# A four-block fp32 chain on one Trainium2 core: the last recurrence over tiles 0 to 7, and slots from a scan

## The chip, the cores and the metric

The kernel runs on one core of one Trainium2 chip. The metric is the device time of one execution in microseconds, from the first to the last instruction with what lies around them; lower is better. It was timed in three executions, and profiled in one more.

## The reference

2048 tokens (4 batches of 512) with 512 features pass four blocks, each added to its input with a gate: an expert MLP chosen by token id, a Hadamard-rotated MLP of width 2048, a decaying recurrence over time, and a routed MLP. The change touches the last two:

```python
# block 3, per batch and feature, over time: k = layernorm(x), v = ctx
no = max(o, u + k); A = exp(o - no); E = exp(u + k - no)
y = (A * p + E * v) / (A * q + E)
# then p, q, o are carried on with decay w
x = x + tanh(g_xattn[1]) * y
# block 4, on xf = layernorm(x)
scores = softmax(xf @ gate_w)
sel = top_k(scores + expert_bias, 2)               # two of 8 experts
order = argsort(sel.reshape(-1), stable=True)      # rows sorted by expert
routed_in = xf[order // 2] * scores_of_sel[order]
h = silu(ragged_dot(routed_in, w1)) * ragged_dot(routed_in, w3)
out = silu(xf @ sw1) * (xf @ sw3) @ sw2            # shared expert
out[order // 2] += ragged_dot(h, w2)
```

## The kernel before

The order of every engine's work is written out by hand; semaphores join the engines. Each engine runs its own queue strictly in order, so an instruction that waits holds all behind it. Tokens lie in 16 tiles of 128. Products are made from a high and a low fp32r part of both factors, three groups of matmuls each.

**The last recurrence and the shared expert share one stage**, the loop `for t in range(TT)` on every engine. A tile t passes: `d_x_shared` (TensorE transposes tile t+1 into bank 0, ScalarE copies the high part dxh and normalizes a later tile into xsd, VectorE subtracts for dxl), `d_up` (24 matmuls, L1332, into banks 2 and 3; it waits for the gate product dmid of tile t-1), the gate (ScalarE's `dsg`, L970, then VectorE's `dmid`, L1731), `d_mid` (transposes of dmid, with dhh on ScalarE and dhl on VectorE) and `d_down` (12 matmuls, L1367), two tiles behind.

Between them lie the four units (128 features each) of the last batch's recurrence, numbers 12 to 15. The table at L39, `KEY_T, VALUE_T, BACK_T`, says in which tile each passes its steps:

- KEY: TensorE transposes the normalized rows xnc (`c_keys`, L1203), VectorE's `front` runs a scan (L1621) and a difference (L1624) into cd, ScalarE's `spread` splits cd in two (L864, L865), GpSimd's `limit` makes a third part (L669).
- VALUE: TensorE transposes values (`c_values`), ScalarE's `exps` makes three exponentials (L882 to L884, with a table load before them, and another before the next dsg), VectorE's `sums` makes five instructions (L1633 to L1639), GpSimd adds (L673), VectorE's `invert` takes a reciprocal (L1643), and GpSimd's last product (L677) gives the unit's output. In GpSimd's queue unit n's L673 and L677 (`finish`) stand before `limit(n + 1)`. ScalarE's `c_norm` makes xnc of the next unit, four instructions at L874, in the same tile.
- BACK: TensorE transposes the output into bank 5 (`c_back`, L1215), and VectorE's `add_out` adds it to the residual (L1649).

On VectorE a tile's order is: `d_x`, `sums`, `d_mul` (dmid), `front`, `add_out`, `d_hid`, `invert`.

Tiles 8 to 15 take their router logits from plain fp32 products (`d_router`, L1344) into columns of bank 5: tiles 8 to 11 at the end of t = 4 to 7, and tiles 12 to 15, whose rows the recurrence ends, in t = LATE = 9. In a tile of BACK_T the router product first waits until `add_out` has read bank 5:

```python
                if HELD - 4 <= t < HELD:
                    if t in BACK_T:
                        pe.wait_ge(s_co, NU - DC + BACK_T.index(t) + 1)
                    d_router(t + 4)
```

**From router to slots.** In tile LATE + 1 VectorE makes softmax and top two (`scores`, `choice`), ending in mask1 (L1768). In tile LATE + 2 TensorE counts, for every token and expert, the tokens ahead of it in 18 matmuls with a triangle and ones (L1384 to L1388), and `places` on VectorE (L1776 to L1797) makes of it each row's slot in the sorted buffer; its last instruction frees the routed part. VectorE's `rows` then makes 32 scaled row tiles (L1615; 4 in tile LATE + 2, then 4 and 3 in each tile), and GpSimd stores each with one indirect DMA (L739). SyncE waits for all 32 and then loads the first routed tile; TensorE waits for it before its last shared `d_down`. Behind the 32 stores GpSimd's queue has the weights of the second expert, and on from there each expert's weights (L593 loads, L600 splits), paced by TensorE's tiles. The routed part has 39 tiles, and the program ends with the gathers of both results.

## Time and profile before

| | |
|---|---|
| three runs | 1429.71, 1430.18, 1434.71 us; median 1430.18 |
| the profiled execution | 1426.54 us, span 1424.9 us, mean granted TensorE clock 0.964 |
| TensorE matmul | 1278.3 us busy, 90% |
| VectorE | 640.9 us, 45% |
| ScalarE | 447.2 us, 31% |
| GpSimd | 384.5 us, 27% |
| chain that ended last | TensorE 61%, issue 14%, GpSimd 10%, DMA 10%, VectorE 3% |

Busy time is each engine's own and overlaps with the others'. The profiled execution ran 3.6 us faster than the median of the timed ones; times read from the trace belong to the former. In the timeline each line gives the start, the time until the end of the group, the engine, the line of the kernel, the operation with its tiles, and in brackets how long the engine had been idle before and what released it. The stage described above runs from about 821 to 995 us, the routed part from 1009 to about 1384 us.

### The profile page before, as it was taken

To read this page: it belongs to the slowest core of one execution; us is meant where nothing else is said; L and a number is where in the kernel's file an instruction comes from. 1 tells how busy PE (TensorE), PEld (TensorE's weight loads), DVE (VectorE), ACT (ScalarE), POOL (GpSimd) and SP (SyncE) were. 2 spreads that over 40 slices of the span, in tenths; PEclk is the share of its full clock that TensorE was granted. 3 is DMA by queue.
4 is the path that set the end of the run, shared out by engine and by line. 5 is a ranking of instruction groups with operands and counts; after the bars stand their busy time and mean duration, and the time that the engine had idled before them with its cause. 6 is when DMAs were issued, how large, how long until landed. Compare 5 with 4: busy or idle time off the path is not lost.

```text
span 1424.9 us, 18510 instructions
## 1 busy us (share of the span) xinstructions
PE 1278.3 (90%) x6269; PEld 1078.1 (76%) x6270; DVE 640.9 (45%) x1066; ACT 447.2 (31%) x755; POOL 384.5 (27%) x314
## 2 busy tenths in 40 slices
PE   3489989999999999999999979999699999998670
PEld 3378877888888888888888868887588888886660
DVE  5423336554436755665465466665132222223116
ACT  1223334333325432543244347542122222222110
POOL 2400011100002311231234142337555220035454
PEclk9999999999999999999999989999799999999795
DMA  8632246564557875794865231235787562257747
GB/s 278 215 101 76 88 137 235 214 227 171 204 192 272 292 281 202 268 338 183 276 265 218 84 85 45 74 116 219 219 229 213 148 192 77 74 158 214 184 136 254
DMA packets 103941, 265.60 MB, mean 186 GB/s; under 512 B 11004, under 2 KB 44872, under 8 KB 91592
## 3 DMA queue, kind: packets, MB, share of 16 engines
q1 hardware_dynamic: 69480, 165.13, 32.6%
q0 software_dynamic: 33968, 99.40, 22.9%
q8 instruction: 37, 0.61, 0.2%
q10 hardware_dynamic: 432, 0.26, 0.1%
q14 instruction: 24, 0.20, 0.0%
HBM read 182.97 MB, written 81.79 MB: 186 GB/s over the span
## 4 chain that ended last, share of the span: by engine, by line
PE 61%; issue 14%; POOL 10%; DMA 10%; DVE 3%; ACT 1%; SPq 1%; POOLq 0%; DVEq 0%; ACTq 0%
PE bank L1166 25%; PE bank L1194 12%; POOL W L600 6%; PE bank L1332 5%; DMA W<-in_L_ffn_w 5%; PE bank L1101 4%; PE bank L1082 4%; PE bank L1121 2%; PE bank L1367 2%; DMA xs_sorted<-xn,slot 1%; POOL fin_low L761 1%; PE bank L1138 1%; POOL xs_sorted L739 1%; DMA fin_high<-y_all,slr 1%; PE bank L1133 1%
## 5 line engine op out<-in xcount | busy, mean ns | idle before, releaser
L1166 PE MATMUL bank<-xTh,G 128*128 128x512 f32 x1024 | 278.5, 397 | 1.8 <-DVE xTl L1577 1.8
L1166 PEld LDWEIGHTS bank<-xTh,G 128*128 128x128 f32 x1024 | 188.8, 188 | 42.6 <-issue 3.4
L1332 PE MATMUL bank<-W,dxh 128*128 (+2 forms) x880 | 203.2, 374 | 0.0
L1332 PEld LDWEIGHTS bank<-W,dxh 128*128 128x128 f32 x880 | 170.2, 193 | 15.7
L1194 PE MATMUL bank<-DN,bhh 128*128 128x512 f32 x512 | 158.2, 390 | 0.0
L1332 PE MATMUL bank<-W,dxl 128*128 (+2 forms) x440 | 116.1, 387 | 29.5 <-POOL W L600 16.6
L1166 PE MATMUL bank<-xTl,G 128*128 128x512 f32 x512 | 137.5, 390 | 0.0
L600 POOL TENSOR_TENSOR W<-wst,W 128x1792 fp32r<-128x1792 f32 (+1 forms) x24 | 101.6, 4233 | 90.5 <-DMA W<-in_L_ffn_w 89.1
L1731 DVE TENSOR_TENSOR dmid<-bank,dsg 128x448 f32<-128x448 f32 x55 | 34.3, 623 | 197.9 <-ACT dsg L970 197.8
L1599 DVE SCALAR_TENSOR_TENSOR bs<-bank,tab,bs 128x512 f32<-128x512 f32 x64 | 47.5, 743 | 161.1 <-PE bank L1166 161.1
L1367 PE MATMUL bank<-W,dhh 112*128 (+1 forms) x440 | 112.6, 398 | 0.0
L1194 PEld LDWEIGHTS bank<-DN,bhh 128*128 128x128 f32 x512 | 96.2, 188 | 21.5 <-issue 1.7
L1166 PEld LDWEIGHTS bank<-xTl,G 128*128 128x128 f32 x512 | 96.1, 188 | 20.9
L1332 PEld LDWEIGHTS bank<-W,dxl 128*128 128x128 f32 x440 | 81.8, 196 | 37.8 <-issue 30.5
L970 ACT ACTIVATE dsg<-bank 128x448 f32<-128x448 f32 x55 | 30.0, 545 | 241.4 <-PE bank L1332 241.4
L1194 PE MATMUL bank<-DN,bhl 128*128 128x512 f32 x256 | 103.7, 405 | 0.0
L1367 PEld LDWEIGHTS bank<-W,dhh 112*128 112x128 f32 x440 | 83.8, 190 | 20.1
L858 ACT ACTIVATE bhh<-bs 128x512 fp32r<-128x512 f32 x64 | 40.3, 630 | 185.3 <-DVE bs L1599 185.3
L1723 DVE TENSOR_TENSOR dxl<-bank,dxh 128x512 fp32r<-128x512 f32 x55 | 37.9, 688 | 113.1 <-ACT dxh L952 113.0
L852 ACT ACTIVATE bs<-bank,tab 128x512 f32<-128x512 f32 x64 | 44.1, 689 | 136.5 <-PE bank L1166 136.5
L529 POOL TENSOR_TENSOR rstd<-vare,cst 128x4 f32<-128x4 f32 x16 | 17.3, 1081 | 230.3 <-DVE vare L1498 230.2
L980 ACT ACTIVATE dys<-bank 128x512 f32<-128x512 f32 x55 | 32.9, 598 | 114.5 <-PE bank L1367 114.5
(229 smaller groups left out, 1960.0 us busy)
## 6 DMA issues: line engine op xcount, KB each, us to landing
G<-gate_up_split SPq DMA_DIRECT2D x48, 1024.0 KB, 7.0
DN<-down_split SPq DMA_DIRECT2D x24, 1024.0 KB, 4.9
wst<-in_L_ffn_w POOLq DMA_DIRECT2D x24, 896.0 KB, 5.6
W<-in_L_ffn_w POOLq DMA_DIRECT2D x24, 896.0 KB, 7.6
gate_up_split<-G SPq DMA_DIRECT2D x16, 1024.0 KB, 7.4
y_all<-dys SPq DMA_DIRECT2D x55, 256.0 KB, 2.0
xs_sorted<-zero POOLq DMA_DIRECT2D x3, 3328.0 KB, 20.9
xsd<-xs_sorted SPq DMA_DIRECT2D x39, 256.0 KB, 3.4
```

What stands on the lines that cost most here:

```text
L600: pool.tensor_tensor(w_place(Wl, slot, p, width), w_rows(p, width), f32(w_place(Wh, slot, p, width)), ALU.subtract)\
L852: act.activation(bs[g % 2][:, :], bank[0][:, :], ACT.Silu, scale=tab[:, T_WGT + g % NK:T_WGT + g % NK + 1]).then_inc(s_bs, 1)
L858: act.activation(bhh[g % 2][:, :], bs[g % 2][:, :], ACT.Copy).then_inc(s_bhh, 1)
L1082: mm = pe.matmul(bank[2 + par][:, :], a[par][:, k, :], w[:, bass.ds(ex[par] * DC + k, 1), :], start=(n == 0), stop=(n == 3 * DC - 1))
L1101: mm = pe.matmul(bank[4 + par][:, :], a[par][:, k, :], w[:, bass.ds(ey * DC + k, 1), :], start=(n == 0), stop=(n == 3 * DC - 1))
L1166: mm = pe.matmul(bank[m][:, :], G[:, c % 2, f, h, m, i, :], a[b % 2][:, i, :], start=(n == 0), stop=(n == 3 * DC - 1))
L1194: mm = pe.matmul(bank[2 + i][:, :], a[g % 2][:, i * P:(i + 1) * P], DN[:, c % 2, f, h, :], start=(k == 0 and n == 0), stop=(k == NK - 1 an ...
L1332: mm = pe.matmul(bank[o][:, 0:width], a[par][:, k, :], w[:, bass.ds(slot, 1), at + k * step:at + k * step + width].rearrange("p a n -> p ( ...
L1367: mm = pe.matmul(bank[4][:, :], a[par][:, k, :], w[0:HP, bass.ds(slot, 1), W_2 + k * D:W_2 + (k + 1) * D].rearrange("p a n -> p (a n)"), s ...
L1599: dve.scalar_tensor_tensor(out=bs[g % 2][:, :], in0=bank[1][:, :], scalar=tab[:, T_WUP + g % NK:T_WUP + g % NK + 1], in1=bs[g % 2][:, :], ...
L1723: dve.tensor_tensor(dxl[t % 2][:, :, :].rearrange("p k n -> p (k n)"), bank[0][:, :], f32(dxh[t % 2][:, :, :]).rearrange("p k n -> p (k n) ...
L1731: dve.tensor_tensor(dmid[t % 2][:, :], bank[3][:, 0:HID], dsg[:, :], ALU.mult).then_inc(s_dmid, 1)
```

## The change

Five edits go together.

1. The recurrence's tables: unit 14 has its keys in tile 3, not 4, and unit 15 in tile 5, not 6; the last output comes back in tile 7 instead of 8.
2. LATE is 8 instead of 9: router tiles 12 to 15, scores, mask, slots and rows all come one tile sooner. `xn_next` keeps ScalarE's normalizing of later tiles in step, and `rows` stops at 32.
3. ScalarE makes xnc of the next unit in the tile of KEY, behind `spread`, not in the tile of VALUE.
4. On VectorE `d_mul` stands ahead of `sums`.
5. mask1 lies expert by expert. A scan with resets counts a token column's hits up to each tile, a subtraction gives those before it, and TensorE needs three matmuls instead of 18.

```diff
--- before.py
+++ after.py
@@ -36,7 +36,7 @@
 LOWEST = -1.0e38
-KEY_T, VALUE_T, BACK_T = (0, 2, 4, 6), (1, 3, 5, 7), (2, 4, 6, 8)
+KEY_T, VALUE_T, BACK_T = (0, 2, 3, 5), (1, 3, 4, 6), (2, 4, 5, 7)
@@ -44,7 +44,7 @@
 HELD = 8
-LATE = 9
+LATE = 8
 NT1 = 2 * TT + E1 - 1
@@ -53,7 +53,7 @@
     ("up", 5), ("router", 8), ("up", 6), ("router", 9), ("up", 7), ("router", 10), ("up", 8), ("router", 11),
-    ("up", 9), ("up", 10), ("router", 12), ("router", 13), ("router", 14), ("router", 15)] + [("up", t) for t in range(11, TT)]
+    ("up", 9), ("router", 12), ("router", 13), ("router", 14), ("router", 15)] + [("up", t) for t in range(10, TT)]
 NTURN = len(TURNS)
@@ -187,9 +187,9 @@
         dmid, dhh, dhl, dys = (dmid0, dmid1), (dhh0, dhh1), (dhl0, dhl1), (dys0, dys1)
-        wst1, wst2, row, sel1, mask1, base1, nt1, tend1, tst1, tex1, tex1_i, tend1_i, slf, slw, slr, rsc = run(
-            WKV, ("wst1", [P, 2048]), ("wst2", [P, 2048]), ("row", [P, 4, D]), ("sel1", [P, TT, E1]), ("mask1", [P, TT + 1, E1]),
-            ("base1", [P, TT + 1, E1]), ("nt1", [P, E1]), ("tend1", [P, E1]), ("tst1", [P, E1]), ("tex1", [P, 48]),
+        wst1, wst2, row, sel1, reset, mask1, upto1, base1, nt1, tend1, tst1, tex1, tex1_i, tend1_i, slf, slw, slr, rsc = run(
+            WKV, ("wst1", [P, 2048]), ("wst2", [P, 2048]), ("row", [P, 4, D]), ("sel1", [P, TT, E1]), ("reset", [P, E1, TT]), ("mask1", [P, E1, TT]), ("upto1", [P, E1, TT]),
+            ("base1", [P, E1 * TT + E1]), ("nt1", [P, E1]), ("tend1", [P, E1]), ("tst1", [P, E1]), ("tex1", [P, 48]),
             ("tex1_i", [P, 48], I32), ("tend1_i", [P, E1], I32), ("slf", [P, 2, TT]), ("slw", [P, 2, TT], I32),
@@ -951,18 +951,22 @@
+            def xn_next(q):
+                if q + 2 < NTURN and TURNS[q + 2] != ("router", HELD + 4):
+                    xn(q + 2)
             def d_x_shared(t):
...
                 d_x(q, t % 2, t - 1)
-                if q + 2 < NTURN and t != LATE:
-                    xn(q + 2)
+                xn_next(q)
...
                 act.activation(dxr[t % 2][:, :, :].rearrange("p k n -> p (k n)"), bank[0][:, :], ACT.Copy).then_inc(s_dxr, 1)
-                xn(q + 2)
+                xn_next(q)
@@ -995,6 +999,8 @@
                     spread(NU - DC + KEY_T.index(t))
+                if t in KEY_T[:-1]:
+                    c_norm(NU - DC + KEY_T.index(t) + 1)
                 if t == LATE:
@@ -1005,8 +1011,6 @@
                     d_x_router(HELD + 7)
-                if t in VALUE_T[:-1]:
-                    c_norm(NU - DC + VALUE_T.index(t) + 1)
                 if t >= 2:
@@ -1379,14 +1383,13 @@
                 if t == LATE + 2:
                     pe.wait_ge(s_mask1, 1)
-                    w = (TT + 1) * E1
-                    pe.matmul(bank[5][:, 0:w], tri, mask1[:, :, :].rearrange("p i e -> p (i e)"), start=True, stop=False)
-                    for j in range(TT):
-                        pe.matmul(bank[5][:, (j + 1) * E1:w].rearrange("p (i e) -> p i e", e=E1), ones,
-                                  mask1[:, j:j + 1, :].broadcast_to([P, TT - j, E1]), start=False, stop=False, skip_group_check=True)
-                    pe.matmul(bank[5][:, 0:w].rearrange("p (i e) -> p i e", e=E1), ones,
-                              mask1[:, TT:TT + 1, :].broadcast_to([P, TT + 1, E1]), start=False, stop=True).then_inc(s_rank1, 1)
+                    w = E1 * TT
+                    pe.matmul(bank[5][:, 0:w], tri, mask1[:, :, :].rearrange("p e i -> p (e i)"), start=True, stop=False)
+                    pe.wait_ge(s_mask1, 2)
+                    pe.matmul(bank[5][:, 0:w], ones, pb[:, :, :].rearrange("p i e -> p (i e)"), start=False, stop=True)
+                    pe.matmul(bank[5][:, w:w + E1], ones, upto1[:, :, TT - 1], start=True, stop=True).then_inc(s_rank1, 1)
                 if t == 0:
@@ -1741,7 +1744,8 @@
                 dve.tensor_copy(lg[:, HELD + 4:TT, :].rearrange("p i e -> p (i e)"), bank[5][:, 4 * E1:(TT - HELD) * E1]).then_inc(s_lr, 1)
-                dve.memset(mask1[:, :, :], 0.0)
+                chain(dve.memset(reset[:, :, :], 1.0))
+                chain(dve.memset(reset[:, :, 0:1], 0.0))
                 dve.wait_ge(s_lr, 5)
@@ -1765,7 +1769,14 @@
                 chain(last)
-                dve.tensor_tensor(mask1[:, 0:TT, :], sel[0][:, :, :], sel[1][:, :, :], ALU.add).then_inc(s_mask1, 1)
+                dve.tensor_tensor(mask1[:, :, :].rearrange("p e i -> p i e"), sel[0][:, :, :], sel[1][:, :, :], ALU.add).then_inc(s_mask1, 1)
+                dve.wait_ge(s_mask1, 1)
+                flat = "p e i -> p (e i)"
+                chain(dve.tensor_tensor_scan(upto1[:, :, :].rearrange(flat), reset[:, :, :].rearrange(flat), mask1[:, :, :].rearrange(flat),
+                                             0.0, ALU.mult, ALU.add))
+                before = pb[:, :, :].rearrange("p i e -> p (i e)")
+                dve.tensor_tensor(before, upto1[:, :, :].rearrange(flat), mask1[:, :, :].rearrange(flat), ALU.subtract).then_inc(s_mask1, 1)
                 for k in range(2):
@@ -1773,8 +1784,10 @@
                 dve.wait_ge(s_rank1, 1)
-                chain(dve.tensor_copy(base1[:, :, :].rearrange("p i e -> p (i e)"), bank[5][:, 0:(TT + 1) * E1]))
-                chain(dve.tensor_tensor(cmp1[:, :, :], base1[:, TT, :].unsqueeze(2).broadcast_to([P, E1, TT]),
+                w = E1 * TT
+                chain(dve.tensor_copy(base1[:, :], bank[5][:, 0:w + E1]))
+                rank = base1[:, 0:w].rearrange("p (e i) -> p i e", i=TT)
+                chain(dve.tensor_tensor(cmp1[:, :, :], base1[:, w:w + E1].unsqueeze(2).broadcast_to([P, E1, TT]),
                                         cst[:, C_THR:C_THR + TT].unsqueeze(1).broadcast_to([P, E1, TT]), ALU.is_gt))
@@ -1782,9 +1795,9 @@
                 chain(dve.tensor_scalar(tst1[:, :], tst1[:, :], float(P), None, ALU.mult))
-                chain(dve.tensor_tensor(base1[:, 0:TT, :], base1[:, 0:TT, :], tst1[:, :].unsqueeze(1).broadcast_to([P, TT, E1]), ALU.add))
+                chain(dve.tensor_tensor(rank, rank, tst1[:, :].unsqueeze(1).broadcast_to([P, TT, E1]), ALU.add))
                 for k in range(2):
-                    chain(dve.tensor_tensor(tmp8[:, :, :], base1[:, 0:TT, :], sel[k][:, :, :], ALU.mult))
+                    chain(dve.tensor_tensor(tmp8[:, :, :], rank, sel[k][:, :, :], ALU.mult))
                     chain(dve.tensor_reduce(slf[:, k, :], tmp8[:, :, :], AX.X, ALU.add))
@@ -1800,7 +1813,7 @@
-                for n in range(rows_done[0], rows_done[0] + count):
+                for n in range(rows_done[0], min(2 * TT, rows_done[0] + count)):
                     t, k = divmod(n, 2)
@@ -1817,8 +1830,6 @@
                     d_x(t + 1)
-                if t in VALUE_T:
-                    sums(NU - DC + VALUE_T.index(t))
                 if t == LATE + 1:
@@ -1826,6 +1837,8 @@
                 d_mul(t)
+                if t in VALUE_T:
+                    sums(NU - DC + VALUE_T.index(t))
                 if t in KEY_T:
```

VectorE in tile 4 before (dxl, lg, dmid of the shared expert; co, cd are `front` of unit 14; xres is `add_out` of unit 13, whose reciprocal lies further up, in tile 3):

```order
L1723 TENSOR_TENSOR dxl_147<-bank,dxh_146 128x512
L1730 COPY lg<-bank 128x8
L1731 TENSOR_TENSOR dmid_153<-bank,dsg 128x448
L1621 SCALAR_TENSOR_TENSOR co<-tab,bank 128x512
L1624 SCALAR_TENSOR_TENSOR cd<-bank,tab,co 128x512
L1649 SCALAR_TENSOR_TENSOR xres<-bank,gates,xres 128x4x128
L1735 TENSOR_TENSOR dhl_158<-bank,dhh_156 112x512
```

VectorE in tile 3 of the change, from dxl of tile 4 on (cev to ce are `sums` of unit 13, co and cd `front` of unit 14, ce at the end the reciprocal of unit 13):

```order
L1726 TENSOR_TENSOR dxl_145<-bank,dxh_144 128x512
L1733 COPY lg<-bank 128x8
L1734 TENSOR_TENSOR dmid_154<-bank,dsg 128x448
L1636 TENSOR_TENSOR cev<-bank,ce_132 128x512
L1638 SCALAR_TENSOR_TENSOR cp<-ce_132,cev 128x512
L1639 SCALAR_TENSOR_TENSOR cq<-ce_132 128x512
L1641 TENSOR_TENSOR cnum<-bank,ce_132 128x512
L1642 TENSOR_TENSOR ce_132<-ce_132,cq 128x512
L1624 SCALAR_TENSOR_TENSOR co<-tab,bank 128x512
L1627 SCALAR_TENSOR_TENSOR cd<-bank,tab,co 128x512
L1738 TENSOR_TENSOR dhl_157<-bank,dhh_155 112x512
L1646 RECIPROCAL ce_132<-ce_132 128x512
```

VectorE in tile 4 of the change (cev to ce_131 are `sums` of unit 14):

```order
L1726 TENSOR_TENSOR dxl_147<-bank,dxh_146 128x512
L1733 COPY lg<-bank 128x8
L1734 TENSOR_TENSOR dmid_153<-bank,dsg 128x448
L1636 TENSOR_TENSOR cev<-bank,ce_131 128x512
L1638 SCALAR_TENSOR_TENSOR cp<-ce_131,cev 128x512
L1639 SCALAR_TENSOR_TENSOR cq<-ce_131 128x512
L1641 TENSOR_TENSOR cnum<-bank,ce_131 128x512
L1642 TENSOR_TENSOR ce_131<-ce_131,cq 128x512
L1652 SCALAR_TENSOR_TENSOR xres<-bank,gates,xres 128x4x128
L1738 TENSOR_TENSOR dhl_158<-bank,dhh_156 112x512
L1646 RECIPROCAL ce_131<-ce_131 128x512
```

Before, a tile had either a unit's sums or another's front and `add_out`. Now tile 3 has sums, front and reciprocal, and tile 4 has `add_out` behind the sums of the unit after.

ScalarE in tiles 0 and 1 before, behind the first dsg (xnc is `c_norm`, ce_131 the parts of unit 12):

```order
L864 ACTIVATE ce_131<-cd 128x512
L865 ACTIVATE ce_131<-cd 128x512
L952 ACTIVATE dxh_144<-bank 128x512
L896 ACTIVATE xsd_142<-xres,nmr,rstd 128x512
L882 ACT_TABLE_LOAD
L882 ACTIVATE ce_131<-ce_131 128x512
L883 ACTIVATE ce_131<-ce_131 128x512
L884 ACTIVATE ce_131<-ce_131,wub 128x512
L970 ACT_TABLE_LOAD
L970 ACTIVATE dsg<-bank 128x448
L975 ACTIVATE dhh_155<-bank 112x512
L874 ACTIVATE xnc<-xres,nmr,rstd 128x128 x4
```

and in the change:

```order
L864 ACTIVATE ce_131<-cd 128x512
L865 ACTIVATE ce_131<-cd 128x512
L874 ACTIVATE xnc<-xres,nmr,rstd 128x128 x4
L952 ACTIVATE dxh_144<-bank 128x512
L896 ACTIVATE xsd_142<-xres,nmr,rstd 128x512
L882 ACT_TABLE_LOAD
L882 ACTIVATE ce_131<-ce_131 128x512
L883 ACTIVATE ce_131<-ce_131 128x512
L884 ACTIVATE ce_131<-ce_131,wub 128x512
L974 ACT_TABLE_LOAD
L974 ACTIVATE dsg<-bank 128x448
```

The four xnc instructions of unit 13 have moved from behind the second dsg and dhh to ahead of the exponentials and that dsg.

## Rows read from the trace of the kernel before

**Rows 1.** Waits after 900 us: engine and line, waited for, us in total, times, longest.
```profile
POOL pace L580 <- PE bank L1332: 125.9, 2, 103.1
```

**Rows 2.** Timeline of TensorE at the turn from shared to routed tiles.
```profile
992.99 2.02 PE L1367 MATMUL bank<-W,dhh 112*128 112x512 f32 x8
1009.47 1.09 PE L1303 MATMUL bank<-cst,xsd 128*128 128x128 f32 x4 [14.45 <-issue]
```

**Rows 3.** Timeline of GpSimd, 955 to 1003 us: the indirect stores.
```profile
957.47 1.48 POOL L739 DMA_INDIRECT xs_sorted<-row,slw  x1 [22.65 <-DVE row L1615]
...
1000.46 0.96 POOL L739 DMA_INDIRECT xs_sorted<-row,slw  x1 [0.30 <-issue]
```

**Rows 4.** Timeline of VectorE, 944.5 to 956 us: mask to slots.
```profile
944.61 0.29 DVE L1768 TENSOR_TENSOR mask<-sel,sel 128x128 f32<-128x128 f32 x1
...
946.52 0.69 DVE L1723 TENSOR_TENSOR dxl<-bank,dxh 128x512 fp32r<-128x512 f32 x1
949.30 0.30 DVE L1776 COPY base<-bank 128x136 f32<-128x136 f32 x1 [2.08 <-PE bank L1388]
...
954.86 0.19 DVE L1797 CAST tex_i<-tex 128x48 int32<-128x48 f32 x1
```

**Rows 5.** Timeline of TensorE: up products of tiles 2, 3, 5, 8 and 9.
```profile
844.46 1.86 PE L1332 MATMUL bank<-W,dxl 128*128 128x456 f32 x4 [6.47 <-DVE dmid L1731]
846.12 2.62 PE L1332 MATMUL bank<-W,dxh 128*128 128x456 f32 x8
...
855.90 1.07 PE L1332 MATMUL bank<-W,dxl 128*128 128x456 f32 x4
856.81 1.82 PE L1332 MATMUL bank<-W,dxh 128*128 128x456 f32 x8
...
878.51 1.07 PE L1332 MATMUL bank<-W,dxl 128*128 128x456 f32 x4
...
910.60 1.06 PE L1332 MATMUL bank<-W,dxl 128*128 128x448 f32 x4
...
919.59 1.06 PE L1332 MATMUL bank<-W,dxl 128*128 128x448 f32 x4
```

**Rows 6.** Stretches: start and end, length, busy PE, PEld, DVE, ACT, POOL, PEclk, DMA.
```profile
844.40:846.00 1.60, 1.54 (x4) 1.42 (x5) 1.60 (x2) 0.00 (x0) 0.31 (x1) 0.50 1.28 260
```

**Rows 7.** Timeline of VectorE, 855 to 880 us, tiles 3 and 4.
```profile
860.86 0.69 DVE L1633 TENSOR_TENSOR cev<-bank,ce 128x512 f32<-128x512 f32 x1 [3.09 <-ACT ce L884]
...
865.37 0.61 DVE L1731 TENSOR_TENSOR dmid<-bank,dsg 128x448 f32<-128x448 f32 x1
865.90 0.68 DVE L1735 TENSOR_TENSOR dhl<-bank,dhh 112x512 fp32r<-112x512 f32 x1
866.50 3.34 DVE L1643 RECIPROCAL ce<-ce 128x512 f32<-128x512 f32 x1
...
872.54 1.21 DVE L1621 TENSOR_TENSOR_SCAN co<-tab,bank 128x512 f32<-128x512 f32 x1
...
874.46 0.74 DVE L1649 SCALAR_TENSOR_TENSOR xres<-bank,gates,xres 128x512 f32<-128x512 f32 x1
```

**Rows 8.** Timeline of ScalarE, 836 to 880 us, tiles 1 to 4.
```profile
840.47 0.54 ACT L970 ACTIVATE dsg<-bank 128x448 f32<-128x448 f32 x1
...
857.76 1.28 ACT L882 ACT_TABLE_LOAD   x1
...
862.14 0.55 ACT L970 ACTIVATE dsg<-bank 128x448 f32<-128x448 f32 x1
...
863.06 1.64 ACT L874 ACTIVATE xnc<-xres,nmr,rstd 128x128 f32<-128x128 f32 x4
...
874.57 0.63 ACT L864 ACTIVATE ce<-cd 128x512 f32<-128x512 f32 x1 [2.68 <-DVE cd L1624]
```

**Rows 9.** Timeline of GpSimd, 845 to 860 us, units 12 and 13.
```profile
848.30 1.30 POOL L677 TENSOR_TENSOR cev<-cnum,ce 128x512 f32<-128x512 f32 x1 [3.59 <-issue]
...
854.57 1.56 POOL L669 TENSOR_SCALAR ce<-cd,wlim 128x512 f32<-128x512 f32 x1 [0.96 <-POOL W L600]
```

## The prediction

> **What bounds the kernel now.** I read four views in this order. The waits after 900 us [rows 1] show GpSimd, which prepares the experts' weights, standing 103.1 us for TensorE's up products of the largest expert. So what GpSimd does behind that follows TensorE, both count from the routed start, and whatever moves that start moves the end. TensorE's timeline at the turn [rows 2] gives the start: the last shared products run at 992.99, and the first routed transposes at 1009.47 after 14.45 us of nothing. GpSimd's timeline [rows 3] says what is late there: 32 indirect stores, the first at 957.47, the last at 1000.46 with 0.96 us, so 45 us from the table of slots to the last row, then a load. VectorE's timeline [rows 4] has the table ready at 954.86 + 0.19 = 955.05. The routed start is therefore slots plus 54.4 us, while TensorE ends the shared part near 995.0. **The one number that counts is when the slots are known.** TensorE may lose up to 14 us more than the slots do, unseen.
>
> The four units of the last batch's recurrence run in tiles 0 to 8 before the router's last part. There TensorE waited 6.47 us ahead of tile 2's up product [rows 5], and restarted slowly: 1.86 + 2.62 us for the twelve matmuls that take 1.07 + 1.82 from 855.90 on. The granted clock was 0.50 then [rows 6], the lower of its two levels. A restart after a wait of that size costs 1.6 us.
>
> **The change, part by part.** I follow up(t), the start of tile t's up product, on the time scale of before.
>
> *up(2): 1.1 us sooner.* ScalarE's table reloads and exponentials put gate(1) at 840.47 [rows 8]. The four xnc instructions for unit 13 now stand before them: 863.06 plus 1.64, 1.54 from start to start. gate(1) then ends at 842.55. VectorE's product now goes ahead of sums(12), so it ends near 843.3, not after 4.5 us of sums (860.86 to 865.37 [rows 7]). up(2) starts at 843.4 instead of 844.46.
>
> *up(3): 3.1 later.* sums(12) now starts where the product ends: 843.3 + 4.4, the dhl subtraction 0.6, the reciprocal 3.34 [rows 7], GpSimd's product 1.30 and 0.1 of hand-over [rows 9] give 853.0 for the output of unit 12. TensorE gets to its c_back at 843.4 + 6.6 (5.0 and the slow restart) + 0.4 = 850.4 and waits 2.6. After that wait it restarts low, 1.6. Sum: -1.1 + 2.6 + 1.6 = +3.1, up(3) at 859.0.
>
> *up(5): 16.9 later.* This is the main term. Unit 14's keys come in tile 3 and its sums in tile 4, one tile after unit 13's sums, and three queues chain up: front(14) stands behind sums(13) on VectorE; GpSimd's limit(14) stands behind finish(13), which waits for the reciprocal of unit 13; ScalarE's exponentials wait for limit(14) and tile 4's gate stands behind them; and add_out(13), for which TensorE's router(8) waits, stands behind sums(14). From up(3): up 5.0, gate 0.55, copy and product 0.7, sums 4.45, front 1.95 (872.54 to 874.46), ScalarE's two spreads 1.05 (0.63 each, starting 0.53 apart), xnc 1.55, dhh 0.6, dhl 0.65, reciprocal 3.35, GpSimd's product 1.4, limit 1.6 (854.57), first table load to the gate's end 4.95 (857.76 to 862.14 + 0.55), copy and product 0.65, sums 4.45, add_out 0.75, and some 0.3 of hand-overs: 34.0 us [rows 5, 7 to 9]. Then router(8) and four transposes at the low clock, 2.4 us. up(5) starts at 859.0 + 34.0 + 2.4 = 895.4, against 878.51. TensorE sees two waits in it. Unit 13's output comes 21.3 us into the chain, at 880.3; TensorE is at c_back(13) by 874.8 (up(3) 5.0, 4.1 of transposes and down, 1.0 of wait for sums(13) to leave bank 7, 0.4, up(4) 5.0, 0.3), so 5.5. Then 4.1 of work and 1.7 of slow restart bring it to 886.1, and add_out(13) ends at 893.0: 6.9.
>
> *up(8): 19.4 later.* Before, up(5) to up(8) took 910.60 - 878.51 = 32.1 us. Added: c_back(15), now in tile 7, 0.4; the rest of the slow restart, 0.6; and a wait for unit 15's output. That is ready 11.45 us after up(6) ends (0.4 of table load, gate 0.55, product 0.7, sums 4.45, dhl 0.6, reciprocal 3.35, GpSimd 1.4), and TensorE has 9.95 us of other work in between (4.95 of transposes, down and router, 5.0 of up(7)), so 1.5. up(8) at 895.4 + 34.6 = 930.0.
>
> *One tile less: 9.0 back.* The late router tiles follow tile 8, not 9; that step is 919.59 - 910.60 = 9.0 [rows 5]. On the same step the change stands at 930.0 against 919.59: +10.4.
>
> *Mask to slots: 1.2 back.* Before, places() began 4.69 us after the mask (944.61 to 949.30 [rows 4]), since TensorE ran its 18 matmuls first. Now VectorE does the scan, a subtraction, the six rsc instructions (to 946.52, 1.7) and dxl, and TensorE's three matmuls lie beside them. The trace has no scan of 128: the floor is the 0.29 of the 128-wide mask, the ceiling the 1.21 of the 512-wide scan at 872.54. I take 0.45, near the floor because a quarter of the width is scanned. 0.3 + 0.45 + 0.3 + 1.7 + 0.65 = 3.4, so -1.3; one more memset gives back 0.1. The ends of the scan's cost move the sum by -0.2 or +0.8.
>
> *Rows over five tiles instead of six:* seven per tile as before, GpSimd takes them at 1.27 us each, so nothing. *Leaving TensorE sooner:* the shared part ends near 1011, still 7 us before the first routed row is back, so it costs nothing; without that cover TensorE's own loss of 16 would count.
>
> **Sum:** slots at 955.05 + 10.4 - 1.2 = 964.3, the routed start at 1018.7, everything behind it 9.2 us later. The profiled execution, 1426.54 (its span 1424.9), becomes 1435.7. The runs shown have their median 3.6 us above it, at 1430.18, so I forecast **1439.4**.
>
> The 1.6 us per slow restart comes from one kind of wait. The Trainium skill, "TensorE: Matmul & The Clock Gate", Part 1 on the clock gate, says that the point at which the gate changes is not tied to the kernel and differs from run to run. This trace shows the restart after 6.47 us and nothing of a wait of 2.6 in this stage. By that rule up(3) could start at full clock; of those 1.6 us half is hidden anyway behind ScalarE's exponentials of unit 13, so the sum would be 8.4 instead of 9.2.
>
> **Rivals.**
> *A, faster: the waits stay covered.* If up(8) is less than 10.2 us later, the change wins, as a tile and the places' 1.2 us are all there is to win. The mechanism would be that VectorE, which idles 3 us at a time ahead of each sums [rows 7], and GpSimd take units 13 and 14 without holding c_back(13) and router(8), so that up(8) keeps its old time: -10.2, **1420.0**. For it: VectorE is busy for 45% of the span, and putting the gate product first does take 1 us from the longest wait. Against it: the 34.0 us chain is made of durations that stand in the rows, in queue orders that stand in the code. 0.13.
> *B, no change.* Only one of tile 4's two waits reaches TensorE (exponentials and sums of unit 14 fit beside the first). Then 6.9 + 1.6 us go: +0.7, **1430.9**. 0.20.
> *C, the scan gains nothing.* VectorE, not TensorE, sets the start of places(): a scan at its ceiling and instructions that wait for each other give 4.5 us in place of 3.4: +10.3, **1440.5**. 0.07.
> *D, more of the same.* Two further restarts of 1.6 show, and the rows reach GpSimd's stores a store's 1.27 late: 9.2 + 3.2 + 1.3 = +13.7, **1443.9**. 0.08.
> The forecast as worked out has the remaining 0.52.
>
> **The numbers.** A measurement of this kernel can tell about 0.5%, 7.2 us, from no change: 1423.0 to 1437.3. Slower: forecast 0.52, C, D, less the part of the forecast that ends under 1437.3 (0.03): 0.64. Same: B and that part: 0.23. Faster: A: 0.13. The terms' own bounds (the chain by 3 us either way, the scan, the restart) give 1435.4 to 1443.2; the range goes on down to B and up to D, 1430 to 1444, and leaves out A and the tails.
>
> **What would show it.** In the profile after: waits of TensorE for GpSimd's output near 2.6 us (tile 2), 5.5 (tile 4) and 1.5 (tile 7), one near 7 ahead of the router product of tile 8, and none over 1 us ahead of an up product from tile 3 on; up(8) near 930; the mask's scan near 0.45; slots near 964; an idle stretch of 7 to 8 us instead of 14.45 at the turn. Slots earlier than 955 would make the forecast wrong, and so would a routed part whose length changes by over 2 us.

## The result, and the profile after

The median of seven runs of the change is 1440.92 us (1437.97 to 1447.04), that of seven runs of before 1430.18 us (1427.43 to 1434.71). The ratio is 1.0078, interval 1.0053 to 1.0102: slower by 10.7 us, 0.8%. The forecast was 1439.4. The profiled execution took 1437.97 us (span 1436.2), 11.4 us more than that of before.

Page after: TensorE 1280.4 us busy, VectorE 638.1, ScalarE 447.2, GpSimd 384.6, all within 3 us of before. No engine has more to do, so the loss is waiting. I read the same views as before the change.

TensorE's timeline of the stage, first before, then after (start, time to the end of the group; idle before and releaser in brackets). The first row of each is the up product of tile 0:

```profile
823.73 1.71 PE L1332 MATMUL bank<-W,dxl 128*128 128x456 f32 x4 [1.67 <-DVE xres L1612]
```

```profile
820.60 1.11 PE L1336 MATMUL bank<-W,dxl 128*128 128x456 f32 x4 [1.67 <-DVE xres L1615]
...
839.82 1.86 PE L1336 MATMUL bank<-W,dxl 128*128 128x456 f32 x4 [5.01 <-DVE dmid L1734]
...
849.50 0.63 PE L1219 MATMUL bank<-cst,cev 128*128 128x128 f32 x4 [2.30 <-POOL cev L677]
849.96 0.60 PE L1355 MATMUL bank<-cst,dmid 128*112 128x128 f32 x4
850.32 1.88 PE L1371 MATMUL bank<-W,dhl 112*128 112x512 f32 x4
...
855.53 1.08 PE L1336 MATMUL bank<-W,dxl 128*128 128x456 f32 x4
...
877.46 1.08 PE L1219 MATMUL bank<-cst,cy_b 128*128 128x128 f32 x4 [5.73 <-POOL cy_b L677]
...
889.72 1.88 PE L1348 MATMUL bank<-rtr,dxr 128*128 128x8 f32 x8 [6.17 <-DVE xres L1652]
...
892.19 1.87 PE L1336 MATMUL bank<-W,dxl 128*128 128x456 f32 x4
...
906.42 1.87 PE L1336 MATMUL bank<-W,dxl 128*128 128x456 f32 x4
...
923.71 0.63 PE L1219 MATMUL bank<-cst,cy_b 128*128 128x128 f32 x4 [1.29 <-POOL cy_b L677]
...
929.03 1.06 PE L1336 MATMUL bank<-W,dxl 128*128 128x448 f32 x4
```

The one wait of 6.47 us in [rows 5] has become 5.01, and behind it stand 2.30, 5.73, 6.17 and 1.29: three are for unit outputs, and 6.17 is for `add_out`. 892.19 is tile 5's up product, 929.03 tile 8's. The stage began 3.1 us sooner in this execution, so I count from tile 0's up product in what follows: the slots come 142.8 us behind it, against 131.3 before.

VectorE's timeline after, mask to slots, answers to [rows 4]: the mask's 0.37, the scan's 0.42, and the last instruction of the places.

```profile
954.02 0.37 DVE L1772 TENSOR_TENSOR mask<-sel,sel 128x128 f32<-128x128 f32 x1
954.42 0.42 DVE L1775 TENSOR_TENSOR_SCAN upto<-reset,mask 128x128 f32<-128x128 f32 x1
954.88 0.29 DVE L1779 TENSOR_TENSOR pb<-upto,mask 128x128 f32<-128x128 f32 x1
...
963.22 0.19 DVE L1810 CAST tex_i<-tex 128x48 int32<-128x48 f32 x1
```

The timeline of all engines from 980 to 1032 us shows what [rows 2, 3] don't have. "remote" stands for a releaser outside the core's own engines and known queues:

```profile
991.19 0.54 ACT L974 ACTIVATE dsg<-bank 128x448 f32<-128x448 f32 x1 [6.64 <-remote]
...
996.96 0.60 ACT L984 ACTIVATE dys<-bank 128x512 f32<-128x512 f32 x1 [3.73 <-remote]
...
1008.50 0.54 ACT L974 ACTIVATE dsg<-bank 128x448 f32<-128x448 f32 x1 [9.48 <-remote]
...
1011.03 1.47 POOL L739 DMA_INDIRECT xs_sorted<-row,slw  x1 [4.46 <-DVE row L1618]
...
1026.26 0.63 PE L1307 MATMUL bank<-cst,xsd 128*128 128x128 f32 x4 [2.20 <-issue]
```

ScalarE stood three times, 19.9 us in all, for nothing the profile can name (I call this the stall). TensorE has gaps of 0.3 to 0.7 us without a named releaser inside the down product from 999.83 on, so ScalarE may not be the only engine that is held up. VectorE's rows stand behind the gate product that needs ScalarE, and GpSimd's 30th store waited 4.46 us for its row. From slots to the routed start (1026.26) it took 62.9 us, where before took 54.4. The routed part and the end took 409.9 us, before 415.4. Slots 11.5 later, a start of the stage 3.1 sooner, 8.4 more from slots to the routed start and 5.5 less behind it sum to the 11.3 us between the two spans.

### The profile page after: what moved, and what is told of

It is laid out like the page before. It is cut to its first block, busy times and chain, and to the rows that moved or that the text cites. A ratio compares the mean times of both kernels' runs of the same rounds, so it can differ in the third digit from the quotient of the medians.

```text
span 1436.2 us, 18457 instructions
## 1 busy us (share of the span) xinstructions
PE 1280.4 (89%) x6239; PEld 1077.7 (75%) x6240; DVE 638.1 (44%) x1069; ACT 447.2 (31%) x755; POOL 384.6 (27%) x314
## 4 chain that ended last, share of the span: by engine, by line
PE 58%; issue 14%; POOL 9%; DMA 8%; DVE 4%; another core or an unknown queue 3%; ACT 2%; SPq 1%; POOLq 0%; ACTq 0%; DVEq 0%
PE bank L1170 24%; PE bank L1198 12%; POOL W L600 6%; DMA W<-in_L_ffn_w 5%; PE bank L1336 4%; PE bank L1105 4%; PE bank L1086 4%; PE bank L1371 2%; PE bank L1125 2%; DVE stats L1505 1%; PE bank L1142 1%; DMA fin_high<-y_all,slr 1%; POOL fin_high L768 1%; DMA xs_sorted<-xn,slot 1%
```

## Experiments

Twelve runs: ten edited kernels, the change once more and the kernel before once more. They stand in three groups, each on a chip of its own (A, B, C), and each is timed against the kernel before on the same chip (medians of before there: 1426.14, 1430.23, 1430.54). "Slots" is from tile 0's up product to the last instruction of the places, "scatter" from there to the first routed transposes, "rest" from there to the span's end. "Late" is a part of slots: from the up product of tile LATE to that of the next tile, with the late router tiles between them. All four are in us, each from one profile.

| kernel | ratio (interval) | slots | late | scatter | rest |
|---|---|---|---|---|---|
| before | | 131.3 | 15.0 | 54.4 | 415.4 |
| the change | 1.0078 (1.0053 to 1.0102) | 142.8 | 14.9 | 62.9 | 409.9 |
| chip A: scan_only | 0.9994 (0.9983 to 1.0005) | 130.4 | 15.0 | 54.2 | 413.4 |
| limit_early | 1.0033 (1.0017 to 1.0049) | 133.4 | 14.9 | 54.6 | 407.5 |
| sums_first | 1.0043 (1.0025 to 1.0061) | 140.1 | 16.5 | 54.6 | 411.0 |
| old_tables | 1.0051 (1.0032 to 1.0070) | 137.6 | 16.5 | 54.3 | 410.9 |
| chip B: norm_moved | 1.0079 (1.0065 to 1.0092) | 140.6 | 16.5 | 56.4 | 413.6 |
| add_early | 1.0057 (1.0036 to 1.0077) | 137.1 | 16.5 | 60.8 | 413.1 |
| limit_and_sums | 1.0025 (1.0007 to 1.0043) | 132.9 | 16.5 | 60.7 | 412.9 |
| gate_first | 0.9997 (0.9980 to 1.0015) | 129.0 | 16.5 | 60.8 | 409.8 |
| chip C: gate_first_norm | 0.9975 (0.9957 to 0.9993) | 129.3 | 17.8 | 60.7 | 418.2 |
| norm_back | 1.0071 (1.0045 to 1.0097) | 142.2 | 18.0 | 59.5 | 417.7 |
| change_again | 1.0101 (1.0063 to 1.0139) | 143.6 | 16.5 | 60.7 | 413.2 |
| before_again | 0.9988 (0.9969 to 1.0008) | 131.3 | 15.0 | 56.5 | 414.7 |

"Late" holds a warning. It is 14.9 or 15.0 where TensorE ran through it at full clock, and 16.5 to 18.0 where it fell to the low level in or just ahead of the down product that follows the router tiles. The same kernel shows both, first the change, then change_again:

```profile
941.75 2.02 PE L1371 MATMUL bank<-W,dhh 112*128 112x512 f32 x8
```

```profile
945.70 3.50 PE L1371 MATMUL bank<-W,dhh 112*128 112x512 f32 x8
```

So a difference in slots of 1.5 us, and up to 3 against norm_back or gate_first_norm, can come from this stretch in one execution and not from an edit.

**limit_early: GpSimd's third part of unit 14 ahead of unit 13's last product.**

```diff
             def finish(n):
...
                 pool.tensor_tensor(cnum[:, :], cnum[:, :], cp[:, 0:512], ALU.add).then_inc(s_cna, 1)
+                if n == NU - 3:
+                    limit(n + 1)
...
             for n in range(NU - DC, NU):
-                limit(n)
+                if n != NU - 2:
+                    limit(n)
```

> The change with one edit: GpSimd makes the third part of unit 14 between its two instructions for unit 13, not behind them. Theory T (the chain of queues in tiles 3 and 4 makes the loss): ScalarE's table load of tile 4 follows cd of unit 14 by some 2 us instead of standing 5.33 us for GpSimd; the 6.17 us that TensorE waits ahead of the router product of tile 8 fall to about 1, the wait for unit 13's output (5.73) stays; the slots come 7 us sooner (near 956.5 against 963.4) and the time falls from 1440.9 to about 1434 (ratio to the kernel before 1.002 to 1.004). Rival R (the loss lies behind the slots, in the stretch from 984 to 1010 where all engines stood in the change's profile): the wait of 6.17 goes all the same, but the time stays at 1440, ratio 1.007 or more.

Timeline of limit_early around tile 4:

```profile
873.07 1.56 POOL L669 TENSOR_SCALAR ce<-cd,wlim 128x512 f32<-128x512 f32 x1 [0.99 <-DVE cd L1630]
...
881.71 1.08 PE L1222 MATMUL bank<-cst,cy_b 128*128 128x128 f32 x4 [5.74 <-POOL cy_b L679]
882.23 0.54 ACT L977 ACTIVATE dsg<-bank 128x448 f32<-128x448 f32 x1
...
888.64 1.06 PE L1351 MATMUL bank<-rtr,dxr 128*128 128x8 f32 x8 [0.20 <-DVE xres L1655]
```

The router's wait is 0.20 in place of 6.17, the one of 5.7 is as it was, and the slots come 9.4 us sooner than in the change. That is theory T, and more than its 7: the slow restarts behind the wait went too. The ratio is the expected one. The ratios themselves are from two chips and differ by the stall as well (below), so the 9.4 us of slots, not the ratios, measure the edit; and for the same reason this run alone doesn't refute rival R, by which the stretch behind the slots makes the loss. limit_and_sums does: it has this edit and the stall, and its ratio is 1.0025.

**add_early: add_out of unit 13 ahead of the gate product in tile 4.**

```diff
+                if t in BACK_T and t in VALUE_T:
+                    add_out(NU - DC + BACK_T.index(t), 5)
                 d_mul(t)
...
-                if t in BACK_T:
+                if t in BACK_T and t not in VALUE_T:
                     add_out(NU - DC + BACK_T.index(t), 5)
```

> The change with add_out of unit 13 ahead of the gate product and the sums of unit 14 on VectorE in tile 4. It takes VectorE's part out of the wait ahead of the router product of tile 8 and leaves the late gate of tile 4. Theory T: the 6.17 us wait goes, 1.5 to 2 us of it come back at the router product or ahead of up(5), which now waits for the gate product, and 2 to 3 us at the output of unit 14, which is not ready when up(5) ends; slots 3 us sooner than in the change, ratio 1.005 to 1.007. Rival B of the prediction (that wait stands alone and is worth 6.9 + 1.6 us): slots 8 us sooner, ratio 1.002 or less.

TensorE in add_early, tiles 4 and 5:

```profile
879.23 1.09 PE L1219 MATMUL bank<-cst,cy_b 128*128 128x128 f32 x4 [4.17 <-POOL cy_b L677]
...
886.68 1.03 PE L1348 MATMUL bank<-rtr,dxr 128*128 128x8 f32 x8 [0.48 <-issue]
...
896.17 0.63 PE L1219 MATMUL bank<-cst,cev 128*128 128x128 f32 x4 [2.61 <-POOL cev L677]
```

The wait ahead of the router product went, 2.61 us came back at unit 14's output as T had it, and the slots came 5.7 us sooner than in the change: between the 3 of T and the 8 of rival B. The ratio is T's. Both edits take away the same wait ahead of the router product, so their 9.4 and 5.7 us don't add up, and with the 1.5 us that "late" differs by, VectorE's order is worth 5.7 to 7.2.

**sums_first: VectorE's old order, in the change.** `sums` stands ahead of `d_mul` again, nothing else (limit_and_sums has this edit and that of limit_early).

```diff
+                if t in VALUE_T:
+                    sums(NU - DC + VALUE_T.index(t))
                 if t == LATE + 1:
                     scores()
...
                 d_mul(t)
-                if t in VALUE_T:
-                    sums(NU - DC + VALUE_T.index(t))
```

> The change with VectorE's old order, the recurrence's sums ahead of the gate product. By the prediction the product first gives 1.1 us at tile 2, with a wait of 2.6 and a slow restart at unit 12's output as its price. Theory T, followed on to the end of the stage: ahead of tile 2's up product TensorE waits some 7.5 us instead of 5.0, but the waits for the outputs of units 12 and 15 (2.30 and 1.29) go and those of tile 4 shrink to about 5 each, so that up(8) and the slots come 4 to 5 us sooner than in the change and the time is about 1436.5, ratio 1.003 to 1.005. Rival (product first is a gain, as at tile 2 alone): the slots come 1 us later, time 1442, ratio 1.008 or more.

As T said, TensorE waits 7.57 us ahead of tile 2's up product, no longer for the outputs of units 12 and 15, 5.33 for unit 13's and 3.84 ahead of the router product. Slots 2.7 us sooner than in the change, where T had 4 to 5; the slow stretch of 1.5 us in "late" makes up the difference to T, for tile 8's up product came 4.2 us sooner. The ratio is in T's range. Edit 4 loses in this kernel what it seems to win at tile 2.

**old_tables: tables, LATE and turns of before; edits 3, 4 and 5 stay.**

```diff
-KEY_T, VALUE_T, BACK_T = (0, 2, 3, 5), (1, 3, 4, 6), (2, 4, 5, 7)
+KEY_T, VALUE_T, BACK_T = (0, 2, 4, 6), (1, 3, 5, 7), (2, 4, 6, 8)
...
-LATE = 8
+LATE = 9
```

> The change with the tables of before (keys 0, 2, 4, 6; values 1, 3, 5, 7; outputs 2, 4, 6, 8), LATE 9 and the old order of turns; the xnc of the next unit in the tile of its keys, the gate product first and the scan stay. Theory T: the six-tile table costs 16 us and gives 9 back, the others are small: waits for unit outputs of 1.0 to 2.3 us in tiles 2, 4, 6 and 8, none of 5 us behind tile 2; slots some 4 us sooner than in the change, time 1435 to 1437, ratio 1.003 to 1.005. Rival (product first and scan are worth what they save): no such waits, slots 2.3 us sooner than before, time 1427.9, ratio 0.998.

Waits at unit outputs of 1.85, 3.15, 1.17 and 1.63 us, none of 5 behind tile 2; slots 5.2 us sooner than in the change and 6.3 later than before. T holds, but for the 3.15 (it had 1.0 to 2.3); the rival (0.998) falls. Of the loss in slots, 11.5 us, the six-tile table with its LATE of 8 is 5.2 as measured, or 6.7 without the slow stretch that only old_tables has in "late". The other 6.3 or 4.8 belong to edits that move no tile. Each is about half.

**scan_only: the kernel before with edit 5 alone**, the hunks of mask1, `places` and TensorE's three matmuls in the diff above.

> The kernel before with the fifth edit alone, the places by a scan. Theory T: from the mask to the start of the places 3.4 us instead of 4.69, slots 1.2 us sooner, all behind it too: time 1429.0, ratio 0.999. Rival C (the scan gains nothing): 4.5 us, time unchanged at 1430. Rival R (18 matmuls gone from TensorE count too): up product of that tile 2.7 us sooner, but the turn idles as much longer, so no more than the 1.2.

Slots 0.9 us sooner, ratio 0.9994: T's 0.999 lies in the interval, and so does no change. The edit is worth what its rows say, and that is too little for the timed runs to show.

**norm_moved: scan_only with edit 3 beside it.** Old tables and sums first; `c_norm` stands behind `spread` in the tile of the keys. Against scan_only (the helper `xn_next` and the bound in `rows` come along and change no order here):

```diff
+                if t in KEY_T[:-1]:
+                    c_norm(NU - DC + KEY_T.index(t) + 1)
...
-                if t in VALUE_T[:-1]:
-                    c_norm(NU - DC + VALUE_T.index(t) + 1)
```

> The kernel before with the scan and with edit 3 alone beside it: ScalarE makes the xnc of the next unit in the tile of its keys; old tables, sums ahead of the gate product. old_tables and sums_first each left a loss of some 6 us that the prediction had no term for. Theory N (edit 3 has a price that I left out): in tiles 1, 3, 5 the xnc no longer fills ScalarE's time after the gate, and in tiles 2 and 4 its 1.6 us stand ahead of dhh and the next dxh, so that up(2) comes 1.5 us later and up(4) and the router product of tile 8 see waits of 2 to 3 us: slots 6 to 8 us later than with the scan alone, time 1431 to 1434 on the scale where the kernel before is 1426.1, ratio 1.004 to 1.006. Rival M (the gate product first is what costs in the old tables): nothing is lost here, ratio 0.999, waits as with the scan alone.

ScalarE in tiles 2 and 3, first scan_only, then norm_moved:

```profile
855.83 0.62 ACT L865 ACTIVATE ce<-cd 128x512 f32<-128x512 f32 x1
856.35 0.58 ACT L975 ACTIVATE dhh<-bank 112x512 fp32r<-112x512 f32 x1
...
862.99 0.54 ACT L970 ACTIVATE dsg<-bank 128x448 f32<-128x448 f32 x1
863.43 0.59 ACT L975 ACTIVATE dhh<-bank 112x512 fp32r<-112x512 f32 x1
863.91 1.64 ACT L874 ACTIVATE xnc<-xres,nmr,rstd 128x128 f32<-128x128 f32 x4
```

```profile
860.51 0.62 ACT L865 ACTIVATE ce<-cd 128x512 f32<-128x512 f32 x1
861.03 1.63 ACT L874 ACTIVATE xnc<-xres,nmr,rstd 128x128 f32<-128x128 f32 x4
862.58 0.57 ACT L979 ACTIVATE dhh<-bank 112x512 fp32r<-112x512 f32 x1
...
869.21 0.55 ACT L974 ACTIVATE dsg<-bank 128x448 f32<-128x448 f32 x1
```

From the split of cd to the next gate ScalarE has no gap in either kernel (the brackets are missing), so the 1.55 us of xnc in that row go straight to the gate: 7.16 us from `spread` to dsg become 8.70. Behind the gate they don't delay it. It shows three times in TensorE's waits: 6.48 becomes 7.58 ahead of tile 2's up product, 1.36 becomes 2.89 ahead of tile 4's, and 0.94 becomes 2.47 ahead of the router product of tile 8, which needs ScalarE's copy dxr from behind the xnc. That is 4.2 us. Most of the other 6 is time at the low clock: the restart of tile 2 lasts longer, behind the wait of 2.47 the router's matmuls take 1.84 in place of 1.03 and the up product behind them is slow too, and "late" is 1.6 longer. The slots come 10.2 us later than with the scan alone and the ratio is 1.0079, above theory N's range. Edit 3 alone costs as much as the whole change.

**norm_back: the change with xnc of units 13 and 15 back in tiles 1 and 4.**

```diff
-                if t in KEY_T[:-1]:
-                    c_norm(NU - DC + KEY_T.index(t) + 1)
+                if t == KEY_T[1]:
+                    c_norm(NU - DC + 2)
...
+                if t in (VALUE_T[0], VALUE_T[2]):
+                    c_norm(NU - DC + VALUE_T.index(t) + 1)
                 if t >= 2:
                     d_y(t - 2)
```

> The change with the xnc of units 13 and 15 back in tiles 1 and 4 and nothing else. Theory N: up(2) 1.5 us sooner than in the change and the gate of tile 6 too, slots 3 us sooner (140 us behind the first up product in place of 142.8), ratio 1.005 to 1.007. Rival: as the change, 1.0078.

Tile 2's wait fell to 3.80 and up(2) came 1.5 us sooner, as expected, but the slots only 0.6 to 1.4 us; the ratio of 1.0071 can't be told from the change's. The profile shows where the gain went. Up to tile 8's up product norm_back is 3.7 us ahead of the change and 3.0 ahead of change_again, as theory N had it. Then TensorE, busy without a gap, ran 16 router matmuls and a down product at the low clock:

```profile
930.20 1.06 PE L1338 MATMUL bank<-W,dxl 128*128 128x448 f32 x4
...
940.15 2.93 PE L1350 MATMUL bank<-rtr,dxr 128*128 128x8 f32 x16
942.92 2.05 PE L1373 MATMUL bank<-W,dhl 112*128 112x512 f32 x4
944.78 3.27 PE L1373 MATMUL bank<-W,dhh 112*128 112x512 f32 x8
```

In the change the same three rows take 1.91, 1.18 and 2.02; the granted clock in norm_back from 940 to 948 us was 0.57. So the two xnc cost some 3 us in this kernel up to tile 8, where edit 3 alone cost 4 us of waits and 6 of mostly slow clock, and whether the slow stretch comes with norm_back's order or with the execution isn't shown. gate_first_norm has the same xnc order and the second longest "late", 17.8; but both profiles are of the longest execution of their kernel, 1446.62 us of five and 1433.77 of twelve.

**limit_and_sums, gate_first, gate_first_norm: is there a version that wins?** The first is limit_early with `sums` ahead of `d_mul`. gate_first is:

```diff
+                if t in VALUE_T[:2]:
+                    d_gate(t)
                 if t in VALUE_T:
                     exps(NU - DC + VALUE_T.index(t))
...
-                d_gate(t)
+                if t not in VALUE_T[:2]:
+                    d_gate(t)
...
-                if t in BACK_T:
+                if t in BACK_T[1:]:
...
+                if t == BACK_T[0]:
+                    pe.wait_ge(s_co, NU - DC)
+                    c_back(NU - DC, 5)
```

with limit_early's edit, and with `sums` behind `d_mul` in tiles 1 and 3 and ahead of it in tiles 4 and 6. gate_first_norm adds norm_back's edit.

> The change with both edits that helped: GpSimd's third part of unit 14 early, and VectorE's sums ahead of the gate product. Theory T: the tile won and the scan are left, one wait of 5.4 us for unit 13's output remains; slots 2 us sooner than before, ratio 0.998 to 0.999. Rival (the two gains are the same gain): as limit_early, slots 2 us later than before, ratio 1.002 to 1.004.

> The change with GpSimd's third part of unit 14 early; in tiles 1 and 3 ScalarE's gate stands ahead of the exponentials (and VectorE's product ahead of the sums), in tiles 4 and 6 the sums stand ahead of the product; TensorE takes unit 12's output behind its down product of tile 0. Theory T: the wait ahead of tile 2's up product falls from 5.0 to about 1, the waits for unit outputs are 1.3 (unit 12) and 4.0 (unit 13), one of 3.6 stands at the values of unit 14; slots 5 to 6 us sooner than before, ratio 0.995 to 0.997. Rival (what is won at tile 2 comes back at unit 12's and 13's outputs, since the sums start no sooner): slots no sooner than in limit_and_sums, ratio 0.998 or more.

> gate_first with the xnc of units 13 and 15 back in the tiles of their predecessors' values (1 and 4), where ScalarE has idle time behind the gate; unit 14's stays in tile 2, since its keys come in tile 3. Theory N (in a tile of keys xnc stands in a row of ScalarE's instructions without a gap, up to the next gate, and costs its 1.6 us each time): slots 2 us sooner than in gate_first (128.9 us behind the first up product there, 131.3 before), ratio 0.995 to 0.998. Rival (edit 3 costs only with sums ahead of the product): no change against gate_first, ratio 0.999 or more.

limit_and_sums missed: slots 0.5 us sooner than limit_early, 1.6 later than before, ratio 1.0025. The rival was right, the two gains are nearly the same gain; without the slow stretch in "late" the second would be worth 2 us. gate_first removed the wait ahead of tile 2's up product (the largest wait of the recurrence's tiles is 4.42, for unit 13's output) and has its slots 2.4 us sooner than before, where I had 5 to 6; no gain can be measured, and the rival's 0.998 or more holds. gate_first_norm has the lowest ratio, 0.9975, interval 0.9957 to 0.9993, inside the range of theory N. A gain over the kernel before isn't settled by it: it is the best of ten kernels, and the kernel before, timed again on the same chip, came out at 0.9988 (0.9969 to 1.0008), which overlaps. Its tile 8 begins 1.2 us sooner than gate_first's, and the low clock in "late" takes that back, so its slots are no sooner. Whether the same gate order wins without the six-tile table wasn't tried.

**change_again and before_again: what belongs to the change.**

> The change as it is, to see what of its profile belongs to it. Theory S (the stall of ScalarE behind the first stores of rows, with 62.9 us from slots to the routed start in place of 54.4, comes and goes with the execution, for any kernel): the waits of 5.0, 2.3, 5.7, 6.2 and 1.3 us in tiles 2 to 7 come again, the time from slots to the routed start lies anywhere from 54 to 63 us. Rival K (the stall belongs to the change's place in the program): 62 to 63 us again. Ratio 1.006 to 1.009 by both.

> The kernel before as it is, profiled beside the others on this chip. Theory S: if the others of this call show ScalarE's stall behind the first row stores, so does this one, and its time from slots to the routed start is 60 to 63 us; if they don't, it is 54.4. Rival K: 54.4 even where the others show the stall. Ratio 1.000, with the spread of single runs.

change_again has its waits of 5.01, 1.77, 4.15, 5.23 and 1.61 us where the change had 5.01, 2.30, 5.73, 6.17 and 1.29, with one of 2.02 for the values of unit 14 and a slow restart behind it. ScalarE's rows for nothing the profile names, first in change_again (with the store that waits), then in before_again (with the routed start):

```profile
1003.01 0.54 ACT L974 ACTIVATE dsg<-bank 128x448 f32<-128x448 f32 x1 [12.84 <-remote]
...
1005.54 1.47 POOL L739 DMA_INDIRECT xs_sorted<-row,slw  x1 [4.86 <-DVE row L1618]
```

```profile
989.64 0.60 ACT L980 ACTIVATE dys<-bank 128x512 f32<-128x512 f32 x1 [3.69 <-remote]
...
994.01 0.54 ACT L970 ACTIVATE dsg<-bank 128x448 f32<-128x448 f32 x1 [3.77 <-remote]
...
998.33 0.60 ACT L980 ACTIVATE dys<-bank 128x512 f32<-128x512 f32 x1 [2.29 <-remote]
...
1014.22 1.09 PE L1303 MATMUL bank<-cst,xsd 128*128 128x128 f32 x4 [9.87 <-issue]
```

The stall stood in all eight profiles of chips B and C and in none of chip A, so it follows the chip or the session more than the kernel: theory S. (In the first comparison it stood in the change's profile and not in before's; whether those two came from one chip I can't tell.) But its price follows the kernel. With LATE at 9 (before_again, norm_moved) the scatter took 56.5 and 56.4 us and no store waited for a row; with LATE at 8 it took 59.5 to 60.8 in six profiles (62.9 in the change's first), and in each one store waited 3.9 to 5.3 us for a row. S had 60 to 63 for before too and was wrong there; K is wrong about the stall itself. So where the stall is, scattering a tile sooner costs 3 to 4 us more than before, where it isn't, nothing (54.6 in limit_early and sums_first). This rests on comparing kernels that differ in more than LATE; no run on a chip with the stall changes LATE alone, and the change wasn't run on chip A.

## Why the prediction was right, point by point

The forecast was slower, 1439.4 against 1430.18, and 1440.92 came. Counted from tile 0's up product:

- *up(2), 1.1 sooner:* 1.5, of which 0.4 is a first product that ran faster. Right, though the gain is not worth having: it pushes the sums back (sums_first).
- *up(3), 3.1 later:* 2.8, with a wait of 2.30 for 2.6. The slow restart of 1.6 came as well, 1.88 us for the four down matmuls at 850.32 that take 1.19 at full clock. TensorE ran its transposes at full clock for 0.8 us and fell low behind them. In change_again the wait there was 1.77, the same four took 1.18, and up(3) came 1.1 us sooner than in the first profile; there the sum of 8.4 is nearer than the 9.2 as far as this restart goes. I had weighed the Trainium skill, "TensorE: Matmul & The Clock Gate", Part 1, by which the gate's point differs from run to run. The traces agree: behind waits of 2.02 and 2.04 us at one place, the values of unit 14, the next up product's first four took 1.87 us in change_again and 1.08 in limit_early.
- *up(5), 16.9 later, the main term:* 16.8, its waits 5.73 and 6.17 for 5.5 and 6.9; in change_again 16.4, with 4.15 and 5.23. limit_early and add_early cut the chain at the two places where it was said to hang, and the time came back. This step is shown.
- *up(8), 19.4 later:* 21.6. The wait for unit 15 was 1.29 for 1.5. What I missed is slow clock: 0.6 us more of the restart at up(5) than I had, and a second slow stretch of 1.6 us up to and in the up product of 906.42, with 1.87 us for four matmuls, though the last wait before it was only 0.96 us, at 904.08. The granted clock was 0.74 from 906 to 911 us. change_again has 1.07 there.
- *one tile less, 9.0 back:* the late router tiles stand between up(8) and up(9), 14.9 us here, 15.0 between up(9) and up(10) before. Right.
- *mask to slots, 1.2 back:* the places began 3.4 us after the mask, as said, and the scan took 0.42 for 0.45. The places themselves took 0.2 us longer, 6.0 for 5.8; alone the edit gave 0.9.
- *slots, 9.2 later:* 11.5 and, in change_again, 12.3. The difference is TensorE's slow clock, in another place each time: around 906.42 in the first profile, and in change_again at up(5) and in the down product at 945.70 that is shown under the table. I had a price for restarts behind long waits and none for the slow stretches without one.
- *rows and scatter, nothing:* wrong. "The routed start is slots plus 54.4 us" holds in before's own profile and on chip A only; the change's scatter took 62.9 and 60.7 us. The step took the scatter for GpSimd's own 1.27 us a store. Its rows come through VectorE behind a gate product, and so through ScalarE.
- *routed part unchanged:* it was 5.5 us shorter, beyond the 2 us I had set. I had said that this would make the forecast wrong. That condition was a bad one: the two profiles of before have 415.4 and 414.7, those of the change 409.9 and 413.2, and fourteen profiles 407.5 to 418.2.
- *idle of 7 to 8 us at the turn:* 2.20 with the stall; 6.12 in limit_early and sums_first, without it.

So the main mechanism and its size were right. That the sum agrees within 2 us is in part luck, from errors of opposite sign: in the first profile 2.3 us of slow clock and 8.4 of scatter missed on one side, 5.5 of routed part and a stage that began 3.1 sooner on the other. Both mechanisms of rival D, which I gave 0.08, came in part: further time at the low clock, and rows that reach their stores late. The cause of the lateness was another, the stall. What stays open: what ScalarE waits for in the stall (no run took anything away there), why the clock falls in some executions while TensorE is busy, why the routed part varies by 10 us, and why, on the chips with the stall, kernels with LATE 8 measure 2 to 6 us less than slots and scatter against before_again add up to.

## What to carry to other kernels

When steps of a pipeline are packed closer, follow one unit through all engines' queues and write the durations in a row: the longest chain, not the busy share, gave this kernel's main term. Before moving an instruction off one engine's tile, look whether it stands in a gap or in a gapless row there; xnc behind the gate didn't delay it, and ahead of it cost 1.1 to 1.5 us of TensorE's time in each of three tiles, with as much again in slow clock behind the longer waits. And cut a chain by what stands in a queue without need of its neighbours (GpSimd's third part of unit 14 behind a product of unit 13): that one edit brought back 9.4 of 11.5 us. Last, before a difference of 1 or 2 us between two profiles is put down to an edit, profile one kernel twice: the change's two profiles differ by 0.8 us in slots and by 1.5 in one stretch of them.

## What the runs showed of the hardware

- ScalarE can stand 2 to 13 us at a time for nothing the profile names, some 15 to 45 us behind the first indirect store, in both kernels, on chips B and C and never on chip A.
- A wait of 2 to 3 us doesn't say whether TensorE goes on at the lower clock level. It did behind 2.02 us (change_again), 2.30 (the change, 1.88 us for four matmuls of 512 columns against 1.18) and 2.47 (norm_moved, 1.84 for eight of the router against 1.03). It did not behind 2.04 twice (limit_early), 2.61 (add_early) and 2.89 (norm_moved).
- TensorE also fell to the low level with no wait over 1 us in the 10 us before: at 906.42 in the change, and in "late" in nine of fourteen profiles, once for 6 to 7 us (estimated from the rows) while it was busy without a gap (norm_back, granted clock 0.57 from 940 to 948 us). The work there is router matmuls of 8 columns and a down product.
- A scan of 128 columns takes 0.42 us, and the sum of two masks 0.37 when written expert by expert, against 0.29 tile by tile.
